# Two attention layers on one core: the first batch's queries staged in vT, and bias heads 2 to 7 loaded later

## The chip, the cores and the metric

The kernel runs on one core of a Trainium2 chip. The metric is the time of the whole program on the device in microseconds. The kernel before took 1788.33 us, the median of 3 runs (1781.52 to 1788.56).

## The reference

The input x is 8 batches of 256 channels by 32 x 32 positions (N = 1024). Two layers follow each other:

```
layer 0: xn   = (x - mean) / sqrt(var + 1e-5) * gamma            over the 256 channels
         q,k,v = w_qkv @ xn, 8 heads of 32 channels
         sim  = q k^T / sqrt(32) + bias[head, i, j]               1024 x 1024 for each head
         y    = w_out @ (softmax(sim) v) + x
layer 1: f, g = Wf y + bf, Wg y + bg (32 channels); h = Wh y + bh
         out  = gamma1 * (h softmax(f^T g)) + y
```

The bias is that of relative positions: a three-layer network on the signed logarithms of the row and column distance, so a table of 8 heads by 63 x 63 values, from which every bias[head, i, j] is taken.

## The kernel before

**Tiling.** The 8 heads are two groups (G = 2) of four (HG = 4). For each batch `element` runs, for each group, 32 row tiles (`A_TILES`) and then 64 column tiles (`SN`). A row tile m multiplies 128 queries by 1024 keys (lines 581, 582); VectorE adds the bias and takes the row maxima (line 1005), ScalarE sums the exponentials (line 819). The row tiles run over half r, then head h, then tile t, so head h of the group is first read at row tile 4h. From the sums come `shift` values, which reach rows 96 and 97 of `q_stack` through `shift_rows` and `shift_to_stack` (line 341), so that the column products (line 602) already hold the softmax's shift. VectorE adds the bias again (line 1019), ScalarE exponentiates (line 836) and TensorE multiplies by `vT` (line 629). Work of layer 1 and of the next batch is laid beside these tiles by hand-written lists (`side_0`, `column_0`, ...: tile number, kind, argument).

**Queries and keys.** They are split in a high and a low part. ScalarE writes the high part to `st` (`high_q0`, `high_k0` for group 0 by halves; `high_q`, `high_k` for group 1), VectorE the low part (`low_q0`, ...). `q_out` and `k_out` store `st` to DRAM (1024 KB), `q_in` (6 transfers of 256 KB) and `k_in` (3 of 512 KB) load it back in another layout to `q_stack` and `k_stack`. For group 0 of batch 0 these are issued by ScalarE's queue (lines 805 to 811), all others by SyncE (SP). In batch 0 `high_q0` waits for `k_stored` (line 721), because keys and queries share `st`, and both query halves go through PSUM bank 5, so the product of the second half waits for `low_q0` of the first.

**The lead-in.** Before batch 0 the table of the bias is computed (4 steps), stored, expanded in DRAM to `bias_lines` (line 369, one transfer for each group, 1008 KB in runs of 128 bytes), and loaded to `bias_lines_sb` by `bias_in` (line 357, 4 transfers of 240 KB for each head). SP issues both expansions, then all 32 loads, heads 0 to 7 in order, and only then enters `element`. VectorE waits for its head's four loads in batch 0 only (line 1002). Meanwhile TensorE makes k0 and q0 (line 450) and waits at the first row tile for all of `q_loaded` and `k_loaded` (lines 575, 576).

**SP's order in `element` of batch 0**: `q_out` and `q_in` of group 1, the load of the next x, `k_out` and `k_in` of group 1, `shift_to_stack` for group 0, then `k_out` and `k_in` of the next batch, and so on. vT is first written by `keep_v` at row tile 3.

Of the kernel before, what the change touches and what calls it, by code (L numbers as in the profile page):

```python
# [8 lines left out]
ACT = mybir.ActivationFunctionType  # L9
AX_X = mybir.AxisListType.X  # L10
F32 = mybir.dt.float32
F32R = mybir.dt.float32r
# [3 lines left out]
HG = P // HD  # L16
# [9 lines left out]
def two_layer_attention(nc, x, mlp_in, rel_in, wqkv_in, gamma_in, ident_in, wout_in, wh_in, wfg_in, bfg_in,  # L26
                        bh, gamma1, out):
    B, C, H, W = x.shape
    N = H * W
    KC = C // P  # L30
    NT = N // P
    HALF = 512
    NHALF = N // HALF
    G = C // P
    ROWS = P // W
# [14 lines left out]
    with ExitStack() as ctx:  # L50
# [48 lines left out]


        squares = st[:].bitcast(F32)
        lnvar = o[:, 1, :]
        rstd = o[:, 1, :]
        attn1 = (probs[:, 0].rearrange("p h n -> p (h n)"), probs[:, 1].rearrange("p h n -> p (h n)"), o[:, 1, :])
# [72 lines left out]
        def need(eng, name, b, n):  # L177
            value = b * per_batch[name] + n
            if value > 0:
                eng.wait_ge(SEMS[name], value)  # L180
# [110 lines left out]
        def split(g, t, half=NHALF - 1):  # L291


            return (1 - t) * NHALF + half + 1 if g == 0 else 2 * NHALF + t + 1

        def through_dram(eng, dram, store_sem):
            eng.dma_start(dram.ap().rearrange("l h d n -> (h d) l n"), st[:].bitcast(F32)).then_inc(store_sem, 16)

        def q_out(eng, b, g):
            need(eng, "lo_ready", b, split(g, 0))  # L300
            need(eng, "q_loaded", b, g * Q_DMAS)
            through_dram(eng, q_dram, q_stored)

        def q_in(eng, b, g, done):

# [8 lines left out]
        def k_out(eng, b, g):  # L314
            need(eng, "lo_ready", b, split(g, 1))
            need(eng, "k_loaded", b, g * K_DMAS)
            through_dram(eng, k_dram, k_stored)

        def k_in(eng, b, g):

            need(eng, "k_stored", b, 16 * (g + 1))
            need(eng, "s_mm", b - 1, (g + 1) * SN)
            for r, part in enumerate((0, 1, 0)):
                eng.dma_start(k_stack[r * HD:(r + 1) * HD, g].bitcast(F32),
                             k_dram.ap()[part].rearrange("h d n -> d h n")).then_inc(k_loaded, 16)
# [3 lines left out]
        @block.sync  # L329
        def _(sp):  # L330
            sp.dma_start(mlp, mlp_in).then_inc(mlp_loaded, 16)
            sp.dma_start(rel_sb, rel_in).then_inc(mlp_loaded, 16)
            sp.dma_start(xn[:], x_dram[0]).then_inc(x_loaded, 16)
            sp.dma_start(wqkvT[:], wqkv_in).then_inc(weights_loaded, 16)
            sp.dma_start(gamma_col[:], gamma_in).then_inc(weights_loaded, 16)

            def shift_to_stack(b, g, r):

                need(sp, "rows_ready", b, g * NHALF + r + 1)
                for part in range(2):  # L340
                    sp.dma_start(q_stack[KS + part:KS + part + 1, g, r].bitcast(F32)
                                 .rearrange("p h (t n) -> p (h t) n", n=P),
                                 shift_rows[part * HM:(part + 1) * HM, r, :].bitcast(F32)).then_inc(rows_loaded, 16)

            def residual_in(b):
                need(sp, "y_stored", b, 0)
                sp.dma_start(x1[:], x_dram[b]).then_inc(res_loaded, 16)

            def result_out(b):
                need(sp, "y_ready", b, KC * NHALF)  # L350
                sp.dma_start(out_dram[b], x1[:]).then_inc(y_stored, 16)


            def bias_in(g):
                for h in range(HG):
                    for yl in range(ROWS):
                        sp.dma_start(bias_lines[yl * W:(yl + 1) * W, g * HG + h],
                                     lines_dram.ap()[g, :, h, yl:yl + NA]
                                     .rearrange("x a w -> x (a w)")).then_inc(lines_loaded[g * HG + h], 16)

            sp.wait_ge(table_ready, MSTEPS)
            sp.dma_start(table_dram.ap()[:, 0:MROWS * DX], table_sb[0:HPT]).then_inc(table_stored, 16)
            sp.dma_start(table_dram.ap()[:, MROWS * DX:DY * DX],
                         table_sb[HPT:2 * HPT, DX:MROWS * DX]).then_inc(table_stored, 16)
            sp.wait_ge(table_stored, 32)
            for g in range(G):
                src = bass.AP(tensor=table_dram.ap().tensor, offset=g * HG * DY * DX,
                              ap=[[1, W], [DX, HG * DY], [1, W]])
                sp.dma_start(lines_dram.ap()[g].rearrange("x h a w -> x (h a) w"), src).then_inc(lines_stored[g], 16)
            for g in range(G):  # L370
                sp.wait_ge(lines_stored[g], 16)
                bias_in(g)

            def element(b, first, last):
                q_out(sp, b, 1)
                q_in(sp, b, 1, ("s_mm", b, 0))
                if not last:

                    need(sp, "v_mm", b, NT)
                    need(sp, "qk_mm", b, split(1, 1))  # L380
                    sp.dma_start(xn[:], x_dram[b + 1]).then_inc(x_loaded, 16)
                k_out(sp, b, 1)
                k_in(sp, b, 1)
                for r in range(NHALF):
                    shift_to_stack(b, 0, r)
                if not last:
                    k_out(sp, b + 1, 0)
                    k_in(sp, b + 1, 0)
                for r in range(NHALF):
                    shift_to_stack(b, 1, r)  # L390
                if not first:
                    result_out(b - 1)
                if not last:
                    q_out(sp, b + 1, 0)
                    q_in(sp, b + 1, 0, ("s_mm", b, SN))
                residual_in(b)

            batches(element)
            result_out(B - 1)
            sp.wait_ge(y_stored, 16 * B)  # L400

        @block.tensor
        def _(pe):
# [8 lines left out]
            def do(kind, arg, b, g, first, last, tail=False):  # L412
# [10 lines left out]
                elif kind in ("q", "k"):  # L423
                    t = ("q", "k").index(kind)
                    if arg == 0:
                        need(pe, "normed", b, KC)

                        if t == 0:
                            need(pe, "bias_added", b, 0)
                        else:  # L430
                            need(pe, "lo_ready", b, split(1, 0))
                    product(arg, 6, lambda k: wqkvT[:, k, t * C + P:t * C + 2 * P], xn, "qk_mm")
                elif kind in ("q0", "k0"):
                    t = ("q0", "k0").index(kind)
                    half, k = divmod(arg, KC)
                    bank = 5 - t * half
                    if k == 0:
                        need(pe, "normed", b, KC)
                        if t == 0 and half:
                            need(pe, "lo_ready", b, split(0, 0, 0))  # L440
                        elif t == 0:
                            need(pe, "lo_ready", b, split(0, 1, 0))
                            need(pe, "y_ready", b - 2, KC * NHALF)
                            need(pe, "o_ready", b - 1, NHALF)
                        elif half:
                            need(pe, "o_ready", b - 1, 1)
                        else:
                            need(pe, "fg_lo", b - 2, 3)
                            need(pe, "v_ready", b - 1, NT)
# [235 lines left out]
        def _(act):  # L685
# [10 lines left out]
            def do(kind, arg, b, g, first, last, tail=False):  # L696
# [13 lines left out]
                    nc.scalar.activation(lnvar, pair(6), ACT.Ln, bias=eps_col[:, 0:1]).then_inc(SEMS["rstd_ready"], 1)  # L710
                elif kind == "high_q":
                    need(act, "qk_mm", b, split(1, 0))
                    need(act, "q_stored", b, 16)
                    nc.scalar.activation(st[:, 0, ::-1], pair(6), ACT.Copy, scale=SCALE).then_inc(SEMS["hi_ready"], 1)
                elif kind == "high_k":
# [2 lines left out]
                    nc.scalar.activation(st[:, 0, :], pair(6), ACT.Copy).then_inc(SEMS["hi_ready"], 1)  # L718
                elif kind == "high_q0":
                    need(act, "qk_mm", b, split(0, 0, arg))  # L720
                    need(act, "k_stored", b, 16)
                    nc.scalar.activation(back(st[:, 0, :], arg * HALF, HALF, N), psum[:, 5, :], ACT.Copy,
                                         scale=SCALE).then_inc(SEMS["hi_ready"], 1)
                elif kind == "high_k0":
                    need(act, "qk_mm", b, split(0, 1, arg))
# [78 lines left out]
            do("rstd", 1, 0, 1, True, False)  # L804
            for kind, arg in (("high_k0", 0), ("high_k0", 1), ("high_q0", 0), ("high_q0", 1)):
                do(kind, arg, 0, 1, True, False)
                if (kind, arg) == ("high_k0", 1):
                    k_out(nc.scalar, 0, 0)
            q_out(nc.scalar, 0, 0)
            k_in(nc.scalar, 0, 0)  # L810
# [44 lines left out]
        def _(dve):  # L855
# [3 lines left out]
            def do(kind, arg, b, g, first, last, tail=False):  # L859
# [17 lines left out]
                                            ALU.subtract).then_inc(SEMS["lo_ready"], 1)  # L877
                elif kind == "low_q0":
                    need(dve, "hi_ready", b, split(0, 0, arg))
                    nc.vector.scalar_tensor_tensor(back(st[:, 1, :], arg * HALF, HALF, N), psum[:, 5, :], SCALE,  # L880
                                                   back(st[:, 0, :], arg * HALF, HALF, N).bitcast(F32),
                                                   ALU.mult, ALU.subtract).then_inc(SEMS["lo_ready"], 1)
                elif kind == "low_k0":
                    cols = slice(arg * HALF, (arg + 1) * HALF)
# [150 lines left out]
def back(ap, start, count, total):  # L1035

    first = total - 1 - start
    stop = first - count
    return ap[:, first:(stop if stop >= 0 else None):-1]
# [72 lines left out]
```

## Time and profile before

| | us |
|---|---|
| median of 3 runs | 1788.33 |
| lowest and highest run | 1781.52, 1788.56 |
| the profiled execution | 1790.26 |
| its span, first to last instruction | 1788.5 |
| TensorE, VectorE, ScalarE busy | 1589.6, 1477.8, 1382.2 |
| TensorE's mean granted clock | 0.934 of full speed |

The span is 1.8 us shorter than the profiled execution's own time, which is 1.9 us above the median. Busy time is averaged over stages; what a stage is worth is read from its own stretch. The page's second part shows the span in 40 slices of 44.7 us: the second slice (44.7 to 89.4 us) has a zero for TensorE, VectorE and ScalarE and a nine for the DMA engines.

### The profile page before, as it was taken

Reading aid. Unit: us, or ns where it says so; the run is one execution under the profiler, and the core shown is the slowest. Engines: PE = TensorE matmul, PEld = TensorE weight load, DVE = VectorE, ACT = ScalarE, POOL = GpSimd, SP = SyncE. Lnnn points to the kernel's source line nnn. Section 1 sums busy time; section 2 is a strip of 40 time slices with the busy share of each in tenths; the row PEclk is TensorE's granted clock in tenths of the full one; section 3 lists DMA queues with packets and bytes.
Section 4 is the critical chain, followed back from the end, with each engine's and each line's share of the span. In section 5 each row is a group of like instructions: output and inputs, shape, how many; then the busy total and the mean of one; then the engine's idle time right before and its main releaser. Section 6 shows DMA issues by size and latency. Waiting matters only on the chain.

```text
span 1788.5 us, 18614 instructions
## 1 busy us (share of the span) xinstructions
PE 1589.6 (89%) x5976; PEld 753.9 (42%) x5976; DVE 1477.8 (83%) x2168; ACT 1382.2 (77%) x2033; POOL 7.1 (0%) x5
## 2 busy tenths in 40 slices
PE   6078899899998999889998999989998999999988
PEld 2043335345353544435453443535444453535424
DVE  3067988898988989898888989899889989899853
ACT  2067889788888878878787888878798887889743
POOL 1000000000000000000000000000000000000000
PEclk9577869999999999999999999999999999999999
DMA  5941204320350203501151203502043203400100
GB/s 129 248 138 36 59 1 132 93 59 1 100 148 1 60 1 107 142 25 35 48 165 37 59 1 107 142 1 60 25 124 101 60 1 90 136 1 0 39 10 23
DMA packets 57257, 122.71 MB, mean 69 GB/s; under 512 B 21428, under 2 KB 22964, under 8 KB 57160
## 3 DMA queue, kind: packets, MB, share of 16 engines
q1 hardware_dynamic: 54344, 115.37, 23.5%
q10 hardware_dynamic: 2816, 6.16, 1.3%
q8 instruction: 47, 0.77, 0.2%
q14 instruction: 50, 0.41, 0.1%
HBM read 78.92 MB, written 44.13 MB: 69 GB/s over the span
## 4 chain that ended last, share of the span: by engine, by line
PE 51%; DVE 24%; issue 18%; DMA 3%; ACT 3%; DVEq 0%; ACTq 0%; SPq 0%
DVE biased L1005 13%; PE psum L527 9%; PE psum L602 9%; PE psum L629 8%; PE psum L581 6%; PE psum L407 6%; DVE biased L1019 5%; PE psum L582 4%; PE psum L450 4%; DMA q_stack<-q_parts 2%; PE psum L460 2%; PE psum L484 1%; ACT probs L836 1%; DVE probs L931 1%; DVE x L954 1%
## 5 line engine op out<-in xcount | busy, mean ns | idle before, releaser
L1005 DVE CUSTOM_DVE_ANT_0 biased<-psum,bias_lines_sb 128x1024 f32<-128x1024 f32 x512 | 617.1, 1222 | 174.1 <-PE psum L582 163.0
L819 ACT ACTIVATE biased<-biased,nmax 128x1024 f32<-128x1024 f32 x512 | 587.4, 1148 | 162.5 <-DVE nmax L1005 157.9
L836 ACT ACTIVATE probs<-biased 128x1024 f32<-128x1024 f32 x512 | 536.8, 1057 | 128.6 <-DVE biased L1019 107.5
L1019 DVE TENSOR_TENSOR biased<-psum,bias_lines_sb 128x1024 f32<-128x1024 f32 x512 | 597.8, 1216 | 45.7 <-PE psum L602 33.4
L602 PE MATMUL psum<-q_stack,k_stack 98*128 98x512 f32 x1024 | 392.8, 490 | 38.5 <-DVE nmax L1005 15.9
L581 PE MATMUL psum<-k_stack,q_stack 96*128 96x512 f32 x512 | 331.1, 647 | 102.5 <-DMA q_stack<-q_parts 46.8
L602 PEld LDWEIGHTS psum<-q_stack,k_stack 98*128 98x128 f32 x1024 | 178.9, 200 | 328.8 <-issue 150.8
L629 PE MATMUL psum<-probs,vT 128*32 128x512 f32 x2048 | 285.1, 627 | 6.2 <-DVE st L886 3.9
L581 PEld LDWEIGHTS psum<-k_stack,q_stack 96*128 96x128 f32 x512 | 100.0, 195 | 287.1 <-DVE nmax L1005 165.8
L582 PE MATMUL psum<-k_stack,q_stack 96*128 96x512 f32 x512 | 210.8, 412 | 0.0
L527 PE MATMUL psum<-probs 128*128 128x512 f32 x384 | 186.6, 592 | 0.0
L582 PEld LDWEIGHTS psum<-k_stack,q_stack 96*128 96x128 f32 x512 | 102.7, 201 | 50.7 <-issue 47.4
L819 ACT ACTIVATION_READ_ACCUMULATOR biased<-biased,nmax 128x1 f32 x512 | 96.0, 188 | 0.0
L450 PE MATMUL psum<-xn,wqkvT 128*128 128x512 f32 x128 | 76.9, 694 | 21.4 <-DVE st L880 7.8
L527 PEld LDWEIGHTS psum<-probs 128*128 128x128 f32 x384 | 72.5, 189 | 46.0 <-issue 36.1
L629 PEld LDWEIGHTS psum<-probs,vT 128*32 128x32 f32 x2048 | 42.6, 109 | 101.3 <-issue 73.5
L761 ACT ACTIVATE probs<-probs,nmax 128x1024 f32<-128x1024 f32 x48 | 54.9, 1144 | 16.4 <-DVE probs L943 15.6
L407 PE MATMUL psum<-xn,wqkvT 128*128 128x512 f32 x128 | 66.3, 599 | 0.0
L460 PE MATMUL psum<-wqkvT,xn 128*128 128x256 f32 x256 | 65.7, 378 | 0.0
L496 PE MATMUL psum<-whT,x 128*128 128x256 f32 x256 | 65.4, 380 | 0.1
L472 PE MATMUL psum<-o,woutT 128*128 128x512 f32 x128 | 64.4, 592 | 0.8 <-ACT o L782 0.8
L527 PE MATMUL psum<-o,probs 128*128 128x512 f32 x128 | 64.8, 592 | 0.0
(78 smaller groups left out, 1090.9 us busy)
## 6 DMA issues: line engine op xcount, KB each, us to landing
q_stack<-q_parts SPq DMA_DIRECT2D x90, 256.0 KB, 5.3
k_stack<-k_parts SPq DMA_DIRECT2D x45, 512.0 KB, 7.3
q_parts<-st SPq DMA_DIRECT2D x15, 1024.0 KB, 3.9
k_parts<-st SPq DMA_DIRECT2D x15, 1024.0 KB, 4.3
xn<-in_x_dram SPq DMA_DIRECT2D x8, 1024.0 KB, 8.9
x<-in_x_dram SPq DMA_DIRECT2D x8, 1024.0 KB, 9.6
out_dram<-x SPq DMA_DIRECT2D x8, 1024.0 KB, 4.1
bias_lines_sb<-bias_lines SPq DMA_DIRECT2D x32, 240.0 KB, 15.1
```

Source lines behind the costliest of these rows:

```text
L407: mm = pe.matmul(psum[0:rows, bank + half, :], lhsT(k), src[:, k, half * HALF:(half + 1) * HALF], start=(k == 0), stop=(k == KC - 1))
L450: mm = pe.matmul(psum[:, bank, :], wqkvT[:, k, t * C:t * C + P], xn[:, k, half * HALF:(half + 1) * HALF], start=(k == 0), stop=(k == KC - 1))
L460: mm = pe.matmul(psum[:, 4 + arg % 2, 0:C], xn[:, k, arg * P:(arg + 1) * P], wqkvT[:, k, 2 * C:3 * C], start=(k == 0), stop=(k == KC - 1))
L527: mm = pe.matmul(psum[:, 4 + 2 * c + half, :], hs[:, t % HS, c * P:(c + 1) * P], attn1[t % 3][:, half * HALF:(half + 1) * HALF], start=(t ...
L581: pe.matmul(psum[:, bank, :], lhsT, keys[:, 0:HALF], start=True, stop=True)
L582: pe.matmul(psum[:, bank + 1, :], lhsT, keys[:, HALF:N], start=True, stop=True).then_inc(SEMS["a_mm"], 1)
L602: mm = pe.matmul(psum[:, bank + i, :], k_stack[:, g, 2 * j + i, t * P:(t + 1) * P], q_stack[:, g, half, 2 * j + i, :], start=True, stop=True)
L629: mm = pe.matmul(psum[h * HD:(h + 1) * HD, 4 + half, :], vT[:, t, (g * HG + h) * HD:(g * HG + h + 1) * HD], probs[:, ((q - PV_LAG) * HP + ...
L819: nc.scalar.activation(biased[:, m % BIASED, :], biased[:, m % BIASED, :], ACT.Exp, scale=-1.0, bias=nmax[:, m:m + 1], accum_out=rowsum[:, ...
L836: nc.scalar.activation(probs[:, n % P_SLOTS], biased[:, n % BIASED, :] .rearrange("p (i n) -> p i n", i=2), ACT.Exp).then_inc(SEMS["probs_ ...
L1005: nc.vector.tensor_tensor_reduce(biased[:, m % BIASED, :], pair(bank_of(g, first, ("rows", m))), bias_lines[:, g * HG + h, a0:a0 + N], -1. ...
L1019: nc.vector.tensor_tensor(biased[:, n % BIASED, :].rearrange("p (i n) -> p i n", i=2), psum[:, bank:bank + 2, :], bias_lines[:, g * HG + 2 ...
```

## The change

In batch 0 the queries of group 0 are staged in `st_first`, a view of `vT`, instead of in `st`; their halves use PSUM banks 6 and 7, each its own, and keys' and queries' products wait for `rstd_ready` in place of each other. `high_q0` of batch 0 no longer waits for `k_stored`; `high_q` (group 1) waits for it in addition. The keys' store is issued after the copy of query half 0 instead of after that of key half 1. SP issues the expansion of group 0, the loads of heads 0 and 1, the expansion of group 1, then waits for all queries and keys of group 0, and issues heads 2 and 3. Heads 4 to 7 follow in `element` of batch 0, between `k_out` and `k_in` of group 1. The diff, cut to its core:

```diff
+        st_first = vT[:].rearrange("p t c -> p (t c)").rearrange("p (l n) -> p l n", l=2).bitcast(F32R)
...
+        def q0_bank(b, half):
+            return 6 + half if b == 0 else 5
+
+        def q0_staged(b):
+            return st_first if b == 0 else st
...
-            through_dram(eng, q_dram, q_stored)
+            through_dram(eng, q_dram, q_stored, q0_staged(b) if g == 0 else st)
...
-            for g in range(G):
-                src = bass.AP(...)
-                sp.dma_start(lines_dram.ap()[g]..., src).then_inc(lines_stored[g], 16)
-            for g in range(G):
-                sp.wait_ge(lines_stored[g], 16)
-                bias_in(g)
+            lines_out(0)
+            bias_in(0)
+            bias_in(1)
+            lines_out(1)
+            need(sp, "q_loaded", 0, Q_DMAS)
+            need(sp, "k_loaded", 0, K_DMAS)
+            bias_in(2)
+            bias_in(3)
...
                 k_out(sp, b, 1)
+                if first:
+                    for h in range(HG, G * HG):
+                        bias_in(h)
                 k_in(sp, b, 1)
...
                         if t == 0:
-                            need(pe, "bias_added", b, 0)
+                            need(pe, "lo_ready", b, split(0, 0))
...
-                    bank = 5 - t * half
+                    bank = q0_bank(b, half) if t == 0 else 5 - half
                     if k == 0:
                         need(pe, "normed", b, KC)
-                        if t == 0 and half:
+                        if b == 0:
+                            need(pe, "rstd_ready", 0, 1)
+                        elif t == 0 and half:
...
                     need(act, "qk_mm", b, split(1, 0))
+                    need(act, "k_stored", b, 16)
                     need(act, "q_stored", b, 16)
...
                     need(act, "qk_mm", b, split(0, 0, arg))
-                    need(act, "k_stored", b, 16)
+                    if b > 0:
+                        need(act, "k_stored", b, 16)
...
-                if (kind, arg) == ("high_k0", 1):
+                if (kind, arg) == ("high_q0", 0):
                     k_out(nc.scalar, 0, 0)
```

`bias_in` now takes a head in place of a group and begins with the wait for its group's expansion (`lines_stored`). `high_q0` and `low_q0` write to `q0_staged(b)` and read the bank `q0_bank(b, arg)`.

## Rows read from the trace of the kernel before

**Rows 1.** The page: busy times of the engines, and the chain's shares by engine.
```profile
PE 1589.6 (89%) x5976; PEld 753.9 (42%) x5976; DVE 1477.8 (83%) x2168; ACT 1382.2 (77%) x2033; POOL 7.1 (0%) x5
...
PE 51%; DVE 24%; issue 18%; DMA 3%; ACT 3%; DVEq 0%; ACTq 0%; SPq 0%
```
**Rows 2.** Chain that ended last, 28 to 110 us: start, length, what.
```profile
31.14 6.21 PE psum L450 x8
...
38.72 6.56 DMA k_parts<-st
45.37 0.60 ACT st L722
...
46.83 3.48 PE psum L450 x4
...
51.69 14.38 DMA q_parts<-st
...
68.36 28.51 DMA q_stack<-q_parts
```
**Rows 3.** Waits, 28 to 98 us: total, times, longest.
```profile
PE psum L581 <- DMA q_stack<-q_parts: 46.8, 1, 46.8
...
PE psum L450 <- DVE st L880: 7.8, 1, 7.8
```
**Rows 4.** Stretches: engines' busy us (instructions), granted clock, DMA share, GB/s.
```profile
31.00:39.35 8.35, 7.91 (x12) 3.12 (x12) 1.38 (x2) 1.19 (x2) 0.00 (x0) 0.69 1.02 135
39.35:97.10 57.75, 3.47 (x4) 1.19 (x5) 1.38 (x2) 1.19 (x2) 0.00 (x0) 0.56 1.03 243
...
52.00:66.00 14.00, 0.00 (x0) 0.00 (x0) 0.00 (x0) 0.00 (x0) 0.00 (x0) 0.55 1.03 292
66.00:97.10 31.10, 0.00 (x0) 0.01 (x1) 0.00 (x0) 0.00 (x0) 0.00 (x0) 0.50 0.97 218
60.00:62.00 2.00, 0.00 (x0) 0.00 (x0) 0.00 (x0) 0.00 (x0) 0.00 (x0) 0.50 1.02 367
```
**Rows 5.** DMA issues from 39.3 to 61 us: count, KB each, median us to landing.
```profile
bias_lines_sb<-bias_lines SPq DMA_DIRECT2D x32, 240.0 KB, 15.1
k_stack<-k_parts ACTq DMA_DIRECT2D x3, 512.0 KB, 24.2
q_parts<-st ACTq DMA_DIRECT2D x1, 1024.0 KB, 14.4
```
**Rows 6.** DMA issues from 115 to 116 us: the store of group 1's queries.
```profile
q_parts<-st SPq DMA_DIRECT2D x1, 1024.0 KB, 3.9
```
**Rows 7.** Timeline of TensorE, 30 to 52 us.
```profile
31.14 7.91 PE L450 MATMUL psum<-xn,wqkvT 128*128 128x512 f32 x12 [3.83 <-DVE xn L869]
46.83 3.47 PE L450 MATMUL psum<-xn,wqkvT 128*128 128x512 f32 x4 [7.78 <-DVE st L880]
```
**Rows 8.** Timeline of ScalarE, 30 to 52 us: the keys' store.
```profile
38.72 0.39 ACTq L297 DMA_DIRECT2D k_parts<-st  x1
```
**Rows 9.** Timeline of SP, 20 to 420 us: issues, merged.
```profile
39.35 21.16 SPq L357 DMA_DIRECT2D bias_lines_sb<-bias_lines  x32
115.12 0.38 SPq L297 DMA_DIRECT2D q_parts<-st  x1
...
126.92 0.38 SPq L297 DMA_DIRECT2D k_parts<-st  x1
133.71 1.27 SPq L324 DMA_DIRECT2D k_stack<-k_parts  x3
136.31 33.30 SPq L341 DMA_DIRECT2D q_stack<-shift_rows  x4
```
**Rows 10.** Timeline of VectorE, 111 to 130 us: row tiles 8 and 12.
```profile
112.72 1.23 DVE L1005 CUSTOM_DVE_ANT_0 biased<-psum,bias_lines_sb 128x1024 f32<-128x1024 f32 x1
...
119.38 1.22 DVE L1005 CUSTOM_DVE_ANT_0 biased<-psum,bias_lines_sb 128x1024 f32<-128x1024 f32 x1 [0.86 <-PE psum L582]
```
**Rows 11.** DMA issues from 136 to 137 us: the first shift rows.
```profile
q_stack<-shift_rows SPq DMA_DIRECT2D x2, 8.0 KB, 6.8
```
**Rows 12.** Timeline of TensorE at 154.8 us: the first column product.
```profile
154.83 0.47 PE L602 MATMUL psum<-q_stack,k_stack 98*128 98x512 f32 x1 [0.23 <-DVE nmax L1005]
```

More of the change, by code:

```diff
@@ L294, in split, with through_dram @@
             return (1 - t) * NHALF + half + 1 if g == 0 else 2 * NHALF + t + 1
-        def through_dram(eng, dram, store_sem):
-            eng.dma_start(dram.ap().rearrange("l h d n -> (h d) l n"), st[:].bitcast(F32)).then_inc(store_sem, 16)
+        def through_dram(eng, dram, store_sem, src):
+            eng.dma_start(dram.ap().rearrange("l h d n -> (h d) l n"), src[:].bitcast(F32)).then_inc(store_sem, 16)
+        def q0_bank(b, half):
+            return 6 + half if b == 0 else 5
+        def q0_staged(b):
+            return st_first if b == 0 else st
         def q_out(eng, b, g):
@@ L316, in k_out @@
             need(eng, "k_loaded", b, g * K_DMAS)
-            through_dram(eng, k_dram, k_stored)
+            through_dram(eng, k_dram, k_stored, st)
         def k_in(eng, b, g):
@@ L351, in result_out, with lines_out, bias_in @@
                 sp.dma_start(out_dram[b], x1[:]).then_inc(y_stored, 16)
[L354 to L359, printed above, removed]
+            def lines_out(g):
+                src = bass.AP(tensor=table_dram.ap().tensor, offset=g * HG * DY * DX,
+                              ap=[[1, W], [DX, HG * DY], [1, W]])
+                sp.dma_start(lines_dram.ap()[g].rearrange("x h a w -> x (h a) w"), src).then_inc(lines_stored[g], 16)
+            def bias_in(h):
+                g, i = divmod(h, HG)
+                sp.wait_ge(lines_stored[g], 16)
+                for yl in range(ROWS):
+                    sp.dma_start(bias_lines[yl * W:(yl + 1) * W, h],
+                                 lines_dram.ap()[g, :, i, yl:yl + NA]
+                                 .rearrange("x a w -> x (a w)")).then_inc(lines_loaded[h], 16)
             sp.wait_ge(table_ready, MSTEPS)
@@ L365, in _ @@
             sp.wait_ge(table_stored, 32)
-            for g in range(G):
-                src = bass.AP(tensor=table_dram.ap().tensor, offset=g * HG * DY * DX,
-                              ap=[[1, W], [DX, HG * DY], [1, W]])
-                sp.dma_start(lines_dram.ap()[g].rearrange("x h a w -> x (h a) w"), src).then_inc(lines_stored[g], 16)
-            for g in range(G):
-                sp.wait_ge(lines_stored[g], 16)
-                bias_in(g)
+            lines_out(0)
[6 more added lines that the diff above has]
+            bias_in(3)
             def element(b, first, last):
@@ L720, in do @@
                     need(act, "qk_mm", b, split(0, 0, arg))
-                    need(act, "k_stored", b, 16)
-                    nc.scalar.activation(back(st[:, 0, :], arg * HALF, HALF, N), psum[:, 5, :], ACT.Copy,
+                    if b > 0:
+                        need(act, "k_stored", b, 16)
+                    nc.scalar.activation(back(q0_staged(b)[:, 0, :], arg * HALF, HALF, N),
+                                         psum[:, q0_bank(b, arg), :], ACT.Copy,
                                          scale=SCALE).then_inc(SEMS["hi_ready"], 1)
@@ L879, in do @@
                     need(dve, "hi_ready", b, split(0, 0, arg))
-                    nc.vector.scalar_tensor_tensor(back(st[:, 1, :], arg * HALF, HALF, N), psum[:, 5, :], SCALE,
-                                                   back(st[:, 0, :], arg * HALF, HALF, N).bitcast(F32),
+                    staged = q0_staged(b)
+                    nc.vector.scalar_tensor_tensor(back(staged[:, 1, :], arg * HALF, HALF, N),
+                                                   psum[:, q0_bank(b, arg), :], SCALE,
+                                                   back(staged[:, 0, :], arg * HALF, HALF, N).bitcast(F32),
                                                    ALU.mult, ALU.subtract).then_inc(SEMS["lo_ready"], 1)
```

## The prediction

> **What bounds the kernel now.** I read the page first. TensorE is busy for 89% of the span and most of the chain that ended last is TensorE and VectorE work [rows 1], so the body of the kernel has no single slack resource to cut. The change barely touches that body: it edits the lead-in of the first batch and the place of the bias loads. So the next view was the chain of waits, cut to 28 to 110 us [rows 2]. There the lead-in is a row of transfers: the products of keys and queries, the store of the keys (38.72, 6.56 us), the second query product (46.83), the store of the queries (51.69, 14.38 us), then the last load into q_stack (issued 68.36, 28.51 us to landing). The list of waits [rows 3] says the same from the engines: TensorE waits 46.8 us for q_stack, and before that 7.8 us for the one staging buffer `st`, which the query halves may not enter until the keys' store has read it. All compute is idle for those 46.8 us, so what shortens them shortens the program.
>
> Why does a 256 KB load take 28 us? The stretches [rows 4] answer: from 39.35 to 97.10 the DMA engines are busy all the time (share 1.03) and move 243 GB/s. That is 57.75 x 0.243 = 14.0 MB, of which the queries and keys are only 2 x 1.05 MB out and 2 x 1.57 MB in. The bulk is `bias_in`: 32 issues of 240 KB [rows 5] = 7.86 MB, beside a remainder of the second `bias_lines` transfer. The ACT queue's transfers share the engines with the SP queue's: a query store takes 14.4 us here [rows 5] and 3.9 us where nothing else runs [rows 6].
>
> **The change part by part.**
>
> 1. Queries staged in vT, in banks 6 and 7. The second query product no longer waits for the first store. TensorE's first twelve records end at 31.14 + 7.91 = 39.05 us; the last four follow at once [rows 7]. They took 3.48 us after their idle time [rows 2]; the four before 39.05 took 7.91 - 6.21 = 1.7 us [rows 2, 7]. I take 1.7, since they follow without a gap: the product ends at 40.8. Before, from its end (46.83 + 3.48 = 50.31) to the issue of the query store (51.69) the copy and the subtraction took 1.4 us [rows 2], so the store is issued at 42.2, at the latest 43.9, against 51.69: 7.8 to 9.5 us earlier. vT is first written by `keep_v`, after row tile 3, which itself waits for q_stack: that cover is free. The new wait of `high_q` for `k_stored` is met long before, since TensorE's first row tile already needs the keys loaded.
>
> 2. The keys' store moves behind the copy of query half 0. The product is ready at 39.05, the copy takes 0.60 us, so the store is issued at 39.7 instead of 38.72 [rows 2, 8]: 1.0 us late. Behind it on ACT stand only the second copy and the query store; it delays neither. Cost 0, or 1.0 us if the keys ended last.
>
> 3. Heads 2 to 7 are taken from in front. Each head is 4 x 240 KB = 0.98 MB, six are 5.90 MB. The engines then have 14.0 - 5.9 = 8.1 MB to move before the first row tile. At the measured 243 GB/s this takes 33.5 us, so TensorE starts at 39.35 + 33.5 = 72.8 us instead of 97.1: **24.3 us saved**. Parts 1 and 3 are one gain, not two: part 1 keeps the engines supplied with query bytes so that part 3 can cash the bytes. Bounds: at the 218 GB/s of the last stretch (66 to 97.1, mostly loads of keys and queries, which stay) 37.3 us, so a saving of 20.4; at the 292 GB/s of 52 to 66 us 27.8 us, so 29.9 [rows 4]. The whole-stretch rate is nearest, as it mixes the same transfers. As a check by the chain: 42.2 + 14.4 (the loaded store) + 14.4 (3.15 MB of loads at 218 GB/s) = 71.0.
>
> 4. `lines_out(1)` moves behind 8 bias issues. Its 1.03 MB goes in 128-byte pieces, and such a stretch ran at 135 GB/s [rows 4]. It now runs beside the query store instead of the keys' store. Those bytes are in both sums. Its result is needed only for heads 4 to 7. Cost 0 beyond part 3.
>
> 5. SP now waits for queries and keys, then issues `bias_in(2)` and `(3)` at 72.8. The 32 issues took 21.16 us [rows 9], so at their mean of 0.66 us eight take 5.3 us. Head 2 (0.98 MB, idle engines, 243 GB/s: 4 us, plus 3.9 us as in a lone store) lands some 8 to 11 us after the start, head 3 four later. They are first read at row tiles 8 and 12, which before began 15.6 and 22.3 us after the first matmul [rows 10]. Cost 0, the margin being 5 us or more. Behind the waiting SP stands `q_out` of group 1, issued 18.0 us after the start before [rows 9]: free.
>
> 6. Heads 4 to 7 (16 issues, 3.93 MB) go between the keys' store of group 1 and its `k_in` and the shift rows. Times from the first matmul T: the store was issued at T+29.8, `k_in` at T+36.6, shift rows at T+39.2 [rows 9]. Sixteen issues take 10.6 us, so SP is done by T+41: `k_in` up to 4 us late, which nobody needs before group 1. What matters is the order in the queue. The store's bytes end near T+35; the bias adds 3.93 / 0.243 = 16.2 us (13.5 to 18.0 at 292 and 218 GB/s), `k_in` needs about 6.5, so the shift rows land near T+59 (T+56 to T+61) instead of T+46 (136.31 + 6.8, [rows 9, 11]). TensorE needs them for its first column product, at 154.83 = T+57.7 [rows 12]. So a wait of 0 to 3 us appears there. VectorE has up to three tiles in hand; I take 0 and keep 3 for the range. Heads 4 to 7 land by T+53, and group 1 reads them only after 64 column tiles that begin at T+57.7.
>
> **Clock.** TensorE stood at 0.50 of full speed, 1.2 GHz, from 66 us to its start [rows 4]; after the change it idles from 41 to 73 us and starts at 1.2 GHz as well. No term.
>
> **The sum.** The profiled execution took 1790.26 us (span 1788.5). 1790.26 - 24.3 = 1766.0. The median of the runs is 1788.33, 1.9 lower, so I forecast **1764 us**. Nothing in later batches is moved, so the shift should be carried to the end.
>
> **The rivals.**
>
> - Cheap bytes. The removed bytes rode partly on spare bandwidth: in 60 to 62 us the engines moved 367 GB/s [rows 4]. Then 5.90 MB are worth 16.1 us, the time is 1772. Against it: the 14 us around that window averaged 292, and the end of the stretch, which decides, ran at 218. Chance 0.10. The Trainium skill ("DMA: Bandwidth & Descriptors", section "Anatomy of one DMA — SWDGE (gpsimd) path") gives the time of a transfer as about 2 us and its bytes by 436 GB/s; that page would make an estimate of 13.5 us saved and 1775 us. The trace disagrees, with 243 GB/s at a DMA share of 1.03.
> - Late shift rows. If bias at this place moves at only the 135 GB/s of the small pieces, 3.93 MB takes 29.1 us and TensorE waits some 14 us at the first column product: 1778 us. Against: its pieces are whole lines, not 128 bytes. Chance 0.06, half of it within 0.5%.
> - Everything latency. If queries and keys ran at their own pace and sharing did not matter, only the 9.5 us of part 1 would be gained, less the 3 of part 6 and the 1 of part 2: 1783, which is within 0.5%. Against: 3.9 us alone, 14.4 us shared [rows 5, 6]. Chance 0.03.
> - Slower than before. The same place as the late shift rows, but worse: the wait outweighs the gain once the bias block takes more than about 40 us, under 99 GB/s. At 75 GB/s it takes 52 us and the wait is 37: 1801 us. No busy row is as slow. Chance 0.03.
> - Larger gain. The query store lands after 3.9 us and the loads follow at 292 GB/s (10.8 us), T = 60 us with 2 us between them: 36 us, 1752. It asks for `bias_in(0)`, `(1)` and `lines_out(1)` to cost nothing. Chance 0.05.
>
> **How the numbers follow.** The forecast has 0.73. Its own bounds are savings of 29.9 and of 20.4 less 3 of waiting: 1758 to 1771. The three runs lie 7.0 us apart, so I add 3.5 on each side: 1755 to 1775, which holds cheap bytes too and leaves out the rest, under 2 in 10. A measurement of this kernel tells about 0.5% (8.9 us) from no change. Faster by more: 0.73 + 0.10 + 0.05 and half of 0.06, less 0.01 for spread: 0.90. Within: 0.07. Slower: 0.03.
>
> **What would show each step.** Query store issued near 42 us on ACT, first row matmul at 70 to 77 us, the wait for q_stack cut from 46.8 to about 32 us. DMA share near 1 up to the start. No wait of VectorE for bias at tiles 8 and 12. The first column product T+58 to T+61, with or without a short wait for a DMA into q_stack. Wrong would be: a start before 67 or after 80 us; gaps in the DMA share before it; a wait of over 5 us for shift rows; a saving at the start that is not found at the end.

## The result and the profile after

The changed kernel took 1764.46 us (median of 4 runs, 1760.01 to 1766.4) against 1788.07 for the kernel before, measured beside it: ratio 0.987, 95% interval 0.984 to 0.990. A second set gave 1761.28 us, 0.985 (0.983 to 0.987). The profiled execution took 1765.2 us, its span is 1763.4 us.

The page of the changed kernel, busy times and the chain's shares (the lines of [rows 1]): the work is the same, the span is shorter.

```profile
PE 1586.7 (90%) x5976; PEld 754.0 (43%) x5976; DVE 1477.6 (84%) x2168; ACT 1382.4 (78%) x2033; POOL 7.1 (0%) x5
...
PE 49%; DVE 24%; issue 18%; DMA 4%; ACT 3%; SPq 1%; DVEq 0%; ACTq 0%
```

The chain from 28 to 110 us (start, length, what), against [rows 2]. The 7.8 us that TensorE waited for `st` are gone, the products of keys and queries are one piece of sixteen records, and the last load takes 12.18 us instead of 28.51.

```profile
34.37 8.75 PE psum L471 x16
44.50 10.51 DMA q_parts<-vT
57.30 12.18 DMA q_stack<-q_parts
```

The waits from 28 to 75 us, and two from 70 to 140 us (total, times, longest), against [rows 3]. The wait for q_stack fell from 46.8 to 26.6 us. The two lines under it are new: TensorE waits for shift rows, and VectorE behind it.

```profile
PE psum L602 <- DMA q_stack<-q_parts: 26.6, 1, 26.6
...
PE psum L623 <- DMA q_stack<-shift_rows: 5.7, 1, 5.7
DVE biased L1045 <- PE psum L623: 5.6, 1, 5.6
```

The timeline of SP (start, length, what) shows the new order of issues, against [rows 9]. The eight issues of heads 2 and 3 begin at 69.50, when queries and keys have landed.

```profile
34.10 0.64 SPq L366 DMA_DIRECT2D bias_lines<-bias_table  x1
42.55 5.82 SPq L372 DMA_DIRECT2D bias_lines_sb<-bias_lines  x8
48.41 0.54 SPq L366 DMA_DIRECT2D bias_lines<-bias_table  x1
69.50 6.12 SPq L372 DMA_DIRECT2D bias_lines_sb<-bias_lines  x8
...
100.32 0.38 SPq L298 DMA_DIRECT2D k_parts<-st  x1
100.75 7.99 SPq L372 DMA_DIRECT2D bias_lines_sb<-bias_lines  x16
...
110.19 36.11 SPq L350 DMA_DIRECT2D q_stack<-shift_rows  x4
```

Stretches, with the columns of [rows 4]: from the first bias issue to the first row matmul, and the last 10 us of it.

```profile
42.55:69.72 27.17, 0.56 (x2) 0.03 (x1) 0.89 (x2) 0.60 (x1) 0.00 (x0) 0.60 1.08 279
...
60.00:69.72 9.72, 0.00 (x0) 0.03 (x1) 0.00 (x0) 0.00 (x0) 0.00 (x0) 0.50 1.16 224
```

The timeline of TensorE gives the two landmarks:

```profile
69.72 0.77 PE L602 MATMUL psum<-k_stack,q_stack 96*128 96x512 f32 x1 [26.61 <-DMA q_stack<-q_parts]
...
132.51 6.02 PE L623 MATMUL psum<-q_stack,k_stack 98*128 98x512 f32 x12 [5.73 <-DMA q_stack<-shift_rows]
```

**Where the 25.1 us came from.** By the two profiled executions the first row matmul came at 69.72 instead of 97.12, 27.4 us earlier. The kernel before has these two lines in its timelines of SP and of TensorE:

```profile
30.96 6.33 SPq L369 DMA_DIRECT2D bias_lines<-bias_table  x2
97.12 0.77 PE L581 MATMUL psum<-k_stack,q_stack 96*128 96x512 f32 x1 [46.82 <-DMA q_stack<-q_parts]
```

The 27.4 us are less than the stretch itself gave: the expansion (the copy of the bias table to `bias_lines`) was issued at 34.10 instead of 30.96. Nothing that the change touches stands in front of it; the first load of x landed 1.5 us later (after 9.3 us instead of 7.8), and the rest of the delay was not followed. I therefore count starts from the expansion's issue: 66.2 us before, 35.6 after, 30.5 less. In the eleven profiled executions below this issue lies between 30.4 and 33.9 us, and differs by 2.0 and 2.7 us between two looks at one kernel, so a shift of this size comes without any edit. Starts scatter too: the four profiles of kernels that issue the same transfers up to the start (the changed kernel and the one with heads 4 to 7 behind the shift rows, twice each) have 35.6, 36.8, 37.4 and 36.6 us. The first column product came 62.8 us after the first row matmul instead of 57.7: 5.1 us given back to the shift rows. What stands at that point is 154.83 - 132.51 = 22.3 us. The rest, 2.8 us, appeared later, where the two kernels are alike, most of it in the last batch. SP's timeline brackets it, first of the kernel before, then of the changed one: at the last load of x the difference is 22.8 us, at the last store 25.1.

```profile
1695.73 0.40 SPq L347 DMA_DIRECT2D x<-in_x_dram  x1
1784.19 0.38 SPq L351 DMA_DIRECT2D out_dram<-x  x1
```

```profile
1672.94 0.40 SPq L356 DMA_DIRECT2D x<-in_x_dram  x1
1759.11 0.38 SPq L360 DMA_DIRECT2D out_dram<-x  x1
```

The stretches between these two landmarks, before and after, have the columns of [rows 4]:

```profile
1695.73:1784.19 88.46, 78.22 (x276) 34.49 (x268) 44.46 (x63) 38.97 (x50) 0.00 (x0) 0.96 0.04 12
1672.94:1759.11 86.17, 75.81 (x276) 33.73 (x268) 44.51 (x63) 39.08 (x50) 0.00 (x0) 1.00 0.04 13
```

The same 276 matmul records took 2.4 us less at a granted clock of 1.00 than at 0.96. It is chance and not the change: the changed kernel's second look took 88.35 us for this stretch, at 0.96. So 2.3 of the 25.1 us are luck of the two profiled executions.

### The profile page after: what moved, and what is told of

It is laid out like the page before. It is cut to its first block, busy times and chain, and to the rows that moved or that the text cites. A ratio compares the mean times of both kernels' runs of the same rounds, so it can differ in the third digit from the quotient of the medians.

```text
span 1763.4 us, 18616 instructions
## 1 busy us (share of the span) xinstructions
PE 1586.7 (90%) x5976; PEld 754.0 (43%) x5976; DVE 1477.6 (84%) x2168; ACT 1382.4 (78%) x2033; POOL 7.1 (0%) x5
## 4 chain that ended last, share of the span: by engine, by line
PE 49%; DVE 24%; issue 18%; DMA 4%; ACT 3%; SPq 1%; DVEq 0%; ACTq 0%
DVE biased L1031 13%; PE psum L548 9%; PE psum L623 9%; PE psum L650 8%; DVE biased L1045 6%; PE psum L602 6%; PE psum L426 5%; PE psum L603 4%; PE psum L471 4%; PE psum L481 2%; PE psum L505 1%; DMA q_stack<-shift_rows 1%; DMA xn<-in_x_dram 1%; ACT probs L860 1%; DVE probs L957 1%
## 5 line engine op out<-in xcount | busy, mean ns | idle before, releaser
L471 PE MATMUL psum<-xn,wqkvT 128*128 128x512 f32 x128 | 74.4, 674 | 14.3 <-issue 6.9
```

What stands on the lines that cost most here:

```text
L471: mm = pe.matmul(psum[:, bank, :], wqkvT[:, k, t * C:t * C + P], xn[:, k, half * HALF:(half + 1) * HALF], start=(k == 0), stop=(k == KC - 1))
```

## The experiments

All ratios are to the kernel before, measured in the same set, with 95% intervals. "Start" is the first row matmul, counted from the expansion's issue.

| kernel | median us | ratio | start | wait for shift rows |
|---|---|---|---|---|
| before | 1787 to 1789 | 1 | 66.2 | 0 |
| changed, first profile | 1764.46 | 0.987 (0.984 to 0.990) | 35.6 | 5.7 |
| changed again | 1761.28 | 0.985 (0.983 to 0.987) | 36.8 | 4.6 |
| queries' buffer alone | 1783.89 | 0.996 (0.994 to 0.999) | 46.9 | 0 |
| the same, second look | 1783.61 | one run | 62.8 | 0 |
| bias order alone | 1764.82 | 0.988 (0.986 to 0.990) | 40.1 | 6.0 |
| heads 4 to 7 behind shift rows | 1759.05 | 0.983 (0.981 to 0.985) | 37.4 | 0 |
| the same again | 1759.22 | 0.984 (0.981 to 0.986) | 36.6 | 0 |
| second expansion late | 1760.77 | 0.985 (0.983 to 0.988) | 35.4 | 5.5 |
| four heads in front | 1771.96 | 0.991 (0.989 to 0.993) | 45.2 | 6.5 |
| buffer alone, expansions apart | 1771.45 | 0.991 (0.989 to 0.993) | 44.3 | 0 |
| late heads and late expansion | 1754.96 | 0.982 (0.980 to 0.984) | 37.3 | 0 |
| the last with one head in front | 1758.58 | 0.984 (0.982 to 0.985) | 34.3 | 0 |

**The changed kernel again.** No edit.

> The changed kernel once more, beside the others. In its first profile the transfer of the expanded lines was issued at 34.1 us instead of 31.0, because the first x load landed later; if that is chance between executions, this run has it near 31 us, the first row matmul 35 to 37 us behind it, and the wait for shift rows of 5 to 6 us again. Time 0.984 to 0.990 of before.

The expansion was issued at 33.15 us. The expectation of 31 was wrong: the kernel before had been looked at on an early one. Start 36.8 and wait 4.6 came as expected within a few tenths.

**The queries' buffer alone.**

```diff
             lines_out(0)
+            lines_out(1)
+            for h in range(G * HG):
+                bias_in(h)
-            bias_in(0)
-            bias_in(1)
-            lines_out(1)
-            need(sp, "q_loaded", 0, Q_DMAS)
-            need(sp, "k_loaded", 0, K_DMAS)
-            bias_in(2)
-            bias_in(3)
...
-                if first:
-                    for h in range(HG, G * HG):
-                        bias_in(h)
```

> Queries in their own buffer, own banks, keys' store moved, but all 32 bias loads in front as before. Theory (the bytes bound the start): the query store is issued 8 to 9 us earlier, its gain is given back in the queue, the first row matmul comes 0 to 3 us earlier, 0.998 to 1.000 of before. Rival (the chain of stores and loads bounds it, at its own pace): 8 to 9.5 us earlier, ratio 0.995. No wait for shift rows in either.

Both missed. The median gained about 5 us, but the twelve runs fall in two groups: four at 1770.27 to 1774.45 (the lower group) and eight at 1783.44 to 1786.82 (the upper group). The profiled run was of the lower group, with a start 19 us earlier than before although all the bias loads are still issued in front. A second look was taken at once.

> Own buffer for the queries alone, a second look, because its 12 executions fell in two groups (1770 to 1775 and 1783 to 1787 us). Theory: in the slower group the loads of keys and queries come when the small packets of the second expansion have already left the SP queue, and share with 240 KB bias loads for their whole length; a slower profile then shows the query store landed after more than 12 us, or q_in issued after 52 us, and the first row matmul near 90 us. Rival: the groups differ somewhere in the later batches, with the start near 77 us in both.

It fell in the upper group. The query store, issued 3.1 us behind the keys' as in the lower one, landed after 7.5 us, so "more than 12" was wrong; q_in was issued at 52.2, as expected, and the start was at 95.9, later than the "near 90". The DMA queues tell them apart (queue q1 is SP's, q10 is ScalarE's; columns: packets, MB, share of the 16 engines). First the profile of the lower group, from 52 to 56.5 us, in the middle of the loads of keys and queries:

```profile
q10 hardware_dynamic: 347, 0.96, 94.3%
q1 hardware_dynamic: 348, 0.04, 10.3%
```

That of the upper group, from 60 to 70 us, in the middle of the same loads:

```profile
q1 hardware_dynamic: 269, 1.36, 61.8%
q10 hardware_dynamic: 266, 0.87, 39.9%
```

The counts of packets are nearly equal in both: in these stretches the engines serve the two queues packet for packet, whatever the packets hold. Where SP's packets are the 128-byte pieces of the expansion, ScalarE's queue has 94% of the engines' share; where they are bias lines (1.36 MB / 269 = 5.1 KB each), it has 40%. The counts are not equal everywhere: from 62 to 74 us of the lower group's profile SP's queue had 461 packets and ScalarE's 336; why is not shown.

In the lower group's profile 4.2 of the 5.24 MB of keys and queries had been moved at 57.5 us, when 99% of the small pieces were gone; in the other 2.1 MB at 51.7 us. The rest had to share with bias lines. So more bias got in before the start: in all, from the first bias issue to the first row matmul, 9.62 MB in 38.5 us against 13.45 MB in 54.3 us. That is 250 and 248 GB/s, so the two groups differ in what is moved before the start and not in the rate. The profiles also differ in the order of the first issues: the keys' store was issued 1.0 us before the first bias load in the lower group's, and at the same time in the other. Whether that decides between the groups is not shown, as there is one profile of each.

This is a rule of the Trainium skill ("DMA: Bandwidth & Descriptors", section "Queues, rings and completion order"): each engine goes round the queues and switches at packet boundaries. The near-equal packet counts of the stretches above agree; the stretch with 461 and 336 does not show it.

**The bias order alone**: SP's part of the change on the kernel before, queries and keys through one buffer.

```diff
+            lines_out(0)
+            bias_in(0)
+            bias_in(1)
+            lines_out(1)
+            need(sp, "q_loaded", 0, Q_DMAS)
+            need(sp, "k_loaded", 0, K_DMAS)
+            bias_in(2)
+            bias_in(3)
...
                 k_out(sp, b, 1)
+                if first:
+                    for h in range(HG, G * HG):
+                        bias_in(h)
```

> Bias loads ordered as in the change, queries and keys still through one buffer. Theory: the bytes are gone from in front, but the query store is issued near 51.5 us as before, so the DMA engines fall idle for part of the time: first row matmul 68 to 74 us instead of 97, 1 to 6 us behind that of the full change counted from the expansion's issue; wait for shift rows 5 to 6 us as in the full change; 0.986 to 0.991 of before. Rival (staging in an own buffer is what pays): less than half of the gain, 0.994 or more.

Start, wait and ratio are as the theory said: 40.1, 6.0, 0.988. Its reason was not: the DMA engines did not fall idle (share 1.11 from the first bias issue to the start). Only ScalarE's queue had nothing moving, from 45.5 to 54.5 us, and SP's packets filled the engines. Of the 30 us at the start, the order alone brings 26.0, the buffer the last 3 to 4.5; of the time the order brings nearly all, and the intervals with and without the buffer overlap. The rival falls. The query store was issued at 51.78, 0.1 us from before, yet the first row matmul came at 73.98, 23.1 us earlier.

**Four heads in front**: a dose of what was taken away.

```diff
-            bias_in(0)
-            bias_in(1)
+            for h in range(HG):
+                bias_in(h)
...
-            bias_in(2)
-            bias_in(3)
```

> The full change, with four heads instead of two loaded in front of the wait: 1.97 MB more before the start. Theory (bytes at 243 GB/s): the first row matmul comes 8.1 us later counted from the expansion's issue (near 44 us instead of 36 to 37), time 7 to 9 us above the changed kernel, 0.990 of before. Rival (cheap bytes, 367 GB/s or less than an even share): 3 to 5.4 us.

Start 45.2, 8.4 to 9.6 us later than in the changed kernel, for 1.97 MB: 8.1 were expected. The time is 7.5 to 10.7 us up on the two medians of the changed kernel. Bias packets in front cost what the prediction charged for them or a little more, 4.2 to 4.8 us for a head where its rate makes 4.0. Cheap bytes fall.

**The second expansion late**: a dose of small packets.

```diff
             bias_in(1)
-            lines_out(1)
...
             bias_in(3)
+            lines_out(1)
```

> The full change, with the second expansion (1.03 MB in 128-byte pieces) issued behind heads 2 and 3, so after the first row matmul. Theory A (bytes and busy share, as in the prediction): these pieces keep the engines busy for about 7 us before the start, so the start comes 5 to 7 us earlier, 0.996 to 0.997 of the changed kernel. Theory B (the two queues take turns packet by packet, and a small packet takes little of a turn): beside them the ACT queue already moved 95% of the bytes, so the start comes 0 to 2 us earlier.

Start 35.4 against 35.6 and 36.8, time 1760.77 against 1761.28: the 5 to 7 us of theory A fall. The dose was smaller than the expectation took it, though: only 0.46 MB of the second expansion was moved before the start of the changed kernel. At 243 GB/s that is 1.9 us, no more than the scatter of the starts. ScalarE's queue settles it. From 60 to 66 us it moves alone in this run:

```profile
q10 hardware_dynamic: 672, 1.26, 104.7%
```

In the same 6 us of the changed kernel's second look it has the small pieces beside it:

```profile
q10 hardware_dynamic: 636, 1.27, 94.9%
q1 hardware_dynamic: 720, 0.09, 15.0%
```

The same data of keys and queries is moved, so here the small pieces cost it nothing: theory B. In the first profile of the changed kernel the 57.3 to 62 us stretch reads:

```profile
q10 hardware_dynamic: 355, 1.04, 94.5%
q1 hardware_dynamic: 369, 0.05, 10.2%
```

**Buffer alone, expansions apart**: all the bias in front, but the second expansion behind heads 0 to 3.

```diff
             lines_out(0)
-            lines_out(1)
-            for h in range(G * HG):
+            for h in range(HG):
+                bias_in(h)
+            lines_out(1)
+            for h in range(HG, G * HG):
                 bias_in(h)
```

(against the kernel with the queries' buffer alone)

> Own buffer for the queries, all 32 bias loads in front of the wait, but the second expansion behind heads 0 to 3 instead of at once behind the first. Theory (turns by packet): keys' and queries' stores now meet large bias packets instead of small ones, share evenly with them, and meet the small ones later; one group of times instead of two. Bytes in front unchanged, so by bytes alone the time is that of the queries' buffer alone in its slower group, 1783 to 1787 us. If small packets shield whatever stands beside them, then q_in, which meets them here, is fast and the start is near 75 to 85 us: 1768 to 1778 us.

The time is 1771.45 us, 0.991, and the start at 44.3, as the second reading said; all six runs are at 1765.76 to 1776.11, none in the upper group. But the expectation takes the bytes in front for unchanged, and they are not. `bias_in(4)` waits for the second expansion, which now stands behind heads 0 to 3 and landed at 82.5 us. SP issued heads 4 to 7 only then, behind the first row matmul at 77.87:

```profile
82.54 8.15 SPq L372 DMA_DIRECT2D bias_lines_sb<-bias_lines  x16
```

From the first bias issue to the start this kernel moved 9.59 MB in 36.3 us, against 13.45 MB in 54.3 us for the upper group of the buffer alone. The 3.9 MB less are heads 4 to 7, 16 us at 243 GB/s, so this run does not tell packets from bytes. In effect it is the kernel with four heads in front over again: that one moved 9.59 MB in 36.8 us and took 1771.96 us. What the run does show is how the two queues share. First from 62 to 66 us, beside bias lines, then from 70 to 76 us, when q_in meets the small pieces:

```profile
q1 hardware_dynamic: 105, 0.51, 58.2%
q10 hardware_dynamic: 105, 0.39, 45.0%
```

```profile
q10 hardware_dynamic: 709, 1.29, 97.0%
q1 hardware_dynamic: 726, 0.09, 15.0%
```

105 and 105 packets, then 709 and 726. ScalarE's queue moves 98 GB/s in the first stretch and 215 in the second. The start is in this queue's hands, so what its packets are paired with sets how fast it goes.

**Heads 4 to 7 behind the first shift rows**: the new wait taken away.

```diff
                 k_out(sp, b, 1)
-                if first:
-                    for h in range(HG, G * HG):
-                        bias_in(h)
                 k_in(sp, b, 1)
-                for r in range(NHALF):
-                    shift_to_stack(b, 0, r)
+                shift_to_stack(b, 0, 0)
+                if first:
+                    for h in range(HG, G * HG):
+                        bias_in(h)
+                shift_to_stack(b, 0, 1)
```

> The full change, with heads 4 to 7 issued behind the first shift rows instead of in front of the load of the keys of group 1. Theory: the wait of 5.7 us before the first column product is the queue of 3.93 MB in front of the shift rows, so it falls to 0 and the run is about 5 us faster than the changed kernel (0.997 of it, 0.984 of before). Rival (that wait stems from the load of keys and x, or is given back at once to VectorE): 0 to 1 us.

> Heads 4 to 7 behind the first shift rows, once more, as the measure for the next two: 0.981 to 0.985 of before, no wait for shift rows.

The wait is gone: the first column product comes 57.1 us after the first row matmul, against 62.8. TensorE's timeline:

```profile
68.09 0.77 PE L602 MATMUL psum<-k_stack,q_stack 96*128 96x512 f32 x1 [27.59 <-DMA q_stack<-q_parts]
...
125.22 0.70 PE L623 MATMUL psum<-q_stack,k_stack 98*128 98x512 f32 x2 [0.23 <-DVE nmax L1031]
```

The shift rows landed after 6.9 us instead of 21.8. The nine runs of this kernel have a median of 1759.2, the eight of the changed one 1762.7. The gain in time, 3.5 us, is near the 5 that were expected, but the sets' intervals overlap. The wait that is gone from both profiles is the firmer evidence.

**Late heads and late expansion**: the last edit and the late second expansion together.

> Heads 4 to 7 behind the first shift rows and the second expansion behind heads 2 and 3. Theory (packet by packet, small packets cost the ACT queue little): same start and same time as with the heads alone, within 2 us. Rival (the expansion's bytes count): 4 us or more faster than that.

The start is no earlier (37.3 against 36.6), as the theory said. The median is 4.3 us lower than that of the heads alone, where the theory said within 2 us and the rival 4 or more. The ranges overlap (1752.35 to 1758.93 and 1753.04 to 1763.86), and no landmark of the first batch shows a gain. In the two profiled executions the difference lies between the first column product and the last load of x, 1535.6 against 1540.5 us, a stretch in which both kernels issue the same work and TensorE was busy for 1422.2 and 1426.4 us with the same number of instructions (mean granted clock 0.96 and 0.95). That speaks for chance in the granted clock and against the rival, but it is not shown. This kernel has the lowest median measured, 0.982 of before.

**One head in front**, on top of that:

```diff
             bias_in(0)
-            bias_in(1)
             need(sp, "q_loaded", 0, Q_DMAS)
             need(sp, "k_loaded", 0, K_DMAS)
+            bias_in(1)
             bias_in(2)
```

> As the last one, with head 0 alone in front of the wait and head 1 behind it. Theory: 0.98 MB of large packets less in front, so the start comes 3.5 to 4.5 us earlier (32 to 33 us behind the expansion's issue), as the step from four heads to two was worth 7 to 9 us; head 1 lands 6 to 8 us after the start and is first read at row tile 4, 7.7 us after it, so VectorE waits 0 to 2 us there: 2 to 4 us faster than with two heads, 0.980 to 0.982 of before. Rival: VectorE's wait for head 1 eats the gain, 0.983.

Start 34.3, 3.0 us earlier than with two heads, a little under the forecast. VectorE did not wait at tile 4 for head 1. The first column product came 59.0 us after the start instead of 57.4, and TensorE's wait for the next x grew from 0.5 to 2.2 us, presumably because this load now queues behind one more head. So about half of the gain at the start was given back in the first batch. The other 1.4 us do not show in the time (1758.58 against 1754.96): the profiled executions lost 7.3 us behind the first column product, where the kernels are alike. Both readings missed, and the time does not decide whether one head in front is worth anything.

## Why the prediction was right, point by point

The time was forecast at 1764 us and measured at 1764.46 and 1761.28. Two terms were off, in opposite directions.

- **What bounds the kernel** was right: the first batch's start on the transfers of queries and keys. The order of the bias alone gave 26 of 30 us.
- **Part 1, the queries' buffer.** The store was to be issued 11.2 us behind the expansion (42.2 - 30.96), and was at 10.4 (44.50 - 34.10). That the buffer and the bytes are one gain held for the changed kernel: 0.988 without the buffer, 0.985 to 0.987 with it, a difference within the intervals; at the start it is 3.4 to 4.5 us. Alone it did more than the 0 to 3 us expected: about 4 us in two thirds of its runs, 17 in the others.
- **Part 2, the keys' store**, cost nothing: it was issued 7.3 us behind the expansion, 7.8 before.
- **Part 3, the start.** 8.1 MB at 243 GB/s, 33.5 us behind the first bias issue, was the mis-sized term: it took 27.2 us. 27.17 x 0.279 = 7.6 MB were moved in it, at 279 GB/s. Of the 6.3 us, 2.3 are the half megabyte that was not moved before the start (the second expansion landed at 74.4 us, after it), and 4.0 are the higher rate. The step that failed is "the engines have so many MB to move before the first row tile", all at one rate. In the kernel before it held because nearly all transfers of both queues had to end before the start, but what must be passed is ScalarE's packets and what SP's queue puts beside them. In the same way part 4 charged the expansion with its bytes, and beside ScalarE's packets they cost nothing that shows. The rate over the whole stretch is not a constant either: it was 243 to 279 GB/s in the profiles named so far and 238 with one head in front, and no run isolates why.
- **Part 5, heads 2 and 3**: no wait of VectorE for bias shows at tiles 8 and 12. Right.
- **Part 6, the shift rows**, taken as 0 with a bound of 3 us, was 5.1 us at the first column product (a wait of 5.7). The place and the mechanism were named; the size was off. The sum itself had a gap: T+35 plus 16.2 and 6.5 us is T+57.7, and the T+59 that it gives has another 1.3 us without a source. The rows landed at 62.3 us after the start, 110.19 + 21.8 - 69.72, against a range of 56 to 61. From the landing of the keys' store they took 24.9 us, where my sum had 22.4. Experiment: with the heads behind them the wait is 0.
- **Clock.** The first row matmul started at 0.50 of full speed in both, as said.
- **The rivals.** Cheap bytes fell with four heads in front. The larger gain was half true: 30.5 us in the stretch. Late shift rows happened at well under half of the rival's price, and not by its condition of 135 GB/s: the stretch from 100.75 to 130.5 us ran at 253.
- **The signs of being wrong.** One was met: a wait of over 5 us for shift rows (5.73, and 4.6 in the second look). Another was close: the start was at 69.72, but with the expansion issued at 30.96 as before, 35.6 us behind it would be 66.6, under the 67 that were named (67.7 by the second look). The wait for q_stack was 26.6 us against about 32, and the first column product came at T+62.8 against T+58 to T+61.

The sum with measured terms: 30.5 - 5.1 = 25.4 us at equal lead-in, against 24.3 forecast. The hit within 1 us is luck: 6 us of error in one place were offset by 5 in another.

## What to carry to other kernels

Before a wait that holds up all engines, look at what the other DMA queue will get through before it, and in what packets: here 128-byte packets beside the loads cost nothing that shows, and packets of 5 KB took more than half of the engines. Check also when the other queue's issues really come, for a wait in front of them changes the bytes as well as their order. Move what is needed later behind the wait, but then look at the small transfers that it lands in front of: 16 KB of shift rows waited behind 3.9 MB. An own buffer that only lets a store start earlier brings little as long as the queue in front of it is full.

## What the runs showed of the hardware that I had not expected

In four stretches two queues shared the engines one packet each: 347 and 348, 269 and 266, 105 and 105, 709 and 726, while the ScalarE queue's share of the engines went from 40% to 97% with the size of the other's packets. Beside 128-byte packets that queue moved 1.27 MB in 6 us, and 1.26 MB with nothing beside it. One kernel whose bias was all issued in front ran in two groups with medians 13.5 us apart (1771.9 and 1785.4): in the profiles of the two, SP's queue got 4.37 and 8.21 MB through before the start.

The sharing does not begin with the issue. In the kernel before the query store was issued at 51.69 us, and from 52 to 57.5 us only SP's queue moved packets; the first one of the store came at 57.9. So 6 of its 14.4 us passed before any sharing. In the kernel with the bias order alone it was 3.4 us (51.78 to 55.2). What it waited for is not shown.
